# A graph network and expert kernel: the edge loop's drain written out, the operand before the gate, all second expert matrices loaded together

## The reference

```
xn  = layernorm(x)
h   = mish([xn[src], xn[dst], edge_attr] @ W1 + b1)
msg = mish(h @ W2 + b2)
agg = segment_sum(msg, dst)
u   = mish([xn, agg] @ W3 + b3)
y   = xn + u @ W4 + b4
x1  = x + layernorm(y) * gamma + beta
xl  = layernorm(x1)
logits = xl @ gate_weight.T              # 16 experts, top 2, softmax of the two
h_e    = silu(xl @ w1[e].T)              # for the tokens routed to expert e
y_e    = mean over these tokens of h_e, times w2[e].T
out    = x1 + sum over a node's two experts of weight * y_e
```

## Time and profile before

| | |
|---|---|
| median of 3 runs | 1175.64 us (1173.95 to 1177.01) |
| profiled execution | 1175.32 us |
| its span in the profile | 1173.7 us |
| mean granted clock of TensorE | 0.945 |
| TensorE busy | 1059.8 us (90%) |
| VectorE busy | 969.4 us (83%) |
| ScalarE busy | 839.6 us (72%) |
| GpSimd busy | 668.8 us (57%) |

### The profile page before, as it was taken

How to read it: one execution, slowest core, us unless ns; L and a number is a source line. 1 busy time by engine, 2 the same in 40 slices (tenths; PEclk the granted TensorE clock), 3 DMA queues, 4 the chain that set the end, 5 groups by cost and what they waited for, 6 DMA issues and landing times. The chain is left out here.

```text
span 1173.7 us, 19190 instructions
## 1 busy us (share of the span) xinstructions
PE 1059.8 (90%) x5670; PEld 882.1 (75%) x5670; DVE 969.4 (83%) x1646; ACT 839.6 (72%) x1028; POOL 668.8 (57%) x522
## 2 busy tenths in 40 slices
PE   2993999999999999999999999999569997599974
PEld 1772788888888888888888888888347776589962
DVE  6751699999999999999999999999857878773366
ACT  3212799999999999999999999999435454344442
POOL 3245777877877877777777877883321211044310
PEclk9996999999999999999999999999779999789975
DMA  6736766666666666666666666663020311635445
GB/s 179 258 113 147 153 132 131 135 131 133 135 130 131 140 131 131 129 137 131 127 131 133 137 132 126 133 131 101 1 73 10 125 35 53 225 91 152 146 133 170
DMA packets 129067, 148.77 MB, mean 127 GB/s; under 512 B 72573, under 2 KB 81158, under 8 KB 128893
## 3 DMA queue, kind: packets, MB, share of 16 engines
q0 software_dynamic: 38576, 97.54, 38.6%
q1 hardware_dynamic: 90381, 50.03, 16.0%
q10 hardware_dynamic: 16, 0.02, 0.0%
HBM read 137.00 MB, written 15.66 MB: 130 GB/s over the span
## 5 line engine op out<-in xcount | busy, mean ns | idle before, releaser
L944 PE MATMUL ps<-W2h,w1l_w3l 128*128 128x512 f32 x1264 | 425.8, 398 | 0.0
L794 POOL DMA_INDIRECT gath<-dst_table,idx_sl x158 | 262.8, 1663 | 54.0 <-issue 47.4
L944 PEld LDWEIGHTS ps<-W2h,w1l_w3l 128*128 128x128 f32 x1264 | 227.1, 189 | 38.1
L944 PE MATMUL ps<-W2l,w1l_w3l 128*128 128x512 f32 x632 | 247.3, 391 | 0.0
L807 POOL DMA_INDIRECT gath<-src_table,idx_sl x156 | 188.2, 1206 | 100.8 <-issue 52.4
L816 POOL TENSOR_TENSOR msg_lo<-act,msg_hi 128x512 fp32r<-128x512 f32 x79 | 126.0, 1595 | 35.5 <-DVE msg_hi L928 35.5
L944 PEld LDWEIGHTS ps<-W2l,w1l_w3l 128*128 128x128 f32 x632 | 118.8, 188 | 26.4
L878 DVE TENSOR_TENSOR agg<-agg,ps 125x512 f32 x166 | 114.1, 688 | 15.2 <-PE ps L988 10.7
L833 ACT ACTIVATE act<-ps 128x1024 f32<-128x1024 f32 x79 | 81.2, 1027 | 38.4 <-PE ps L976 38.4
L908 DVE SCALAR_TENSOR_TENSOR act<-act,ps 128x1024 f32<-128x1024 f32 x79 | 96.0, 1215 | 2.8 <-ACT act L861 2.8
L890 DVE SCALAR_TENSOR_TENSOR act<-act,ps 128x1024 f32<-128x1024 f32 x79 | 96.0, 1215 | 2.1 <-ACT act L852 2.1
(11 more groups left out here) (345 smaller groups left out, 2363.7 us busy)
## 6 DMA issues: line engine op xcount, KB each, us to landing
w_raw<-in_L_ffn_w_dram SPq DMA_DIRECT2D x25, 512.0 KB, 4.6
ea_sl<-ea_scr SPq DMA_DIRECT2D x158, 64.0 KB, 4.2
ea_scr<-in_edge_attr_dram POOLq DMA_DIRECT2D x1, 5000.0 KB
w_late<-in_L_ffn_w_dram SPq DMA_DIRECT2D x7, 512.0 KB, 6.3
w_raw<-in_L_gnn_W_dram SPq DMA_DIRECT2D x3, 1024.0 KB, 11.5
gath<-src_table,idx_sl POOLq DMA_INDIRECT x158
gath<-dst_table,idx_sl POOLq DMA_INDIRECT x158
x_raw<-in_x_dram SPq DMA_DIRECT2D x5, 448.0 KB
```

What stands on the lines that cost most here:

```text
L794: pool.indirect_dma_start(out=gath[:, k, j, :], out_offset=None, in_=dst_table[:, :], in_offset=bass.IndirectOffsetOnAxis(ap=idx_sl[:, p % ...
L944: return nc.tensor.matmul(ps_2[:, p % 2, j, :], part[:, p % 2, d, j * P:(j + 1) * P], weights[:, d, :], start=False, stop=last)
```

## The change

In the edge phase: the one-hot ring has four slots. VectorE's loop ends after step 79, and the rest of its program is a written list. GpSimd makes no lower half of the last two messages. VectorE makes both halves. The sums of the last three visits go to other banks (two in `ps_2`), so four banks are in use. ScalarE copies the first piece of W3 after the last Exp and the other seven behind its last step. GpSimd makes six remainders of W3, VectorE two.

```diff
+        SUM_BANKS = {PAIRS + 1: (ps_2, 0), PAIRS + 2: (ps_2, 1), PAIRS + 3: (ps_1, PAIRS % 2)}
...
-        act_parts = {PAIRS: (0, 1, 2, 3), PAIRS + 1: (4, 5, 6, 7)}
-        dve_parts = {PAIRS + 4: (0,), PAIRS + 5: (1,), PAIRS + 6: (2,), PAIRS + 7: (3,)}
-        pool_parts = {PAIRS + 3: (4, 5, 6, 7)}
+        DRAIN = PAIRS + 1
+        dve_parts, pool_parts = (0, 1), tuple(range(2, 2 * KC))
...
+            last = PAIRS - 1
+            add_sums(last - 3, 1, second)
+            mark(last - 1)
+            old = last - 2
...
+            nc.vector.tensor_tensor(msg_lo[:, ring(old)][:, 0], act2[:, old % A2, 0], f32(msg_hi[:, ring(old)][:, 0]), ALU.subtract).then_inc(S["msg_lo0_ready"], 1)
+            message(last - 1)
+            dve.wait_ge(S["exp2"], PAIRS)
+            nc.vector.tensor_scalar(act2[:, last % A2], act2[:, last % A2], EXP_MAX, 1.0, ALU.min, ALU.add).then_inc(S["inc2"], 1)
+            split(last - 1)
+            mark(last)
+            add_pair(last - 2)
+            mark(last + 1)
+            mark(last + 2)
+            message(last)
+            split(last)
+            mark(last + 3)
+            add_pair(last - 1)
+            for w in dve_parts:
...
+                nc.vector.tensor_tensor(w3l[:, w, :], w_raw[:, w, :], f32(w3h[:, w, :]), ALU.subtract).then_inc(S["w3_lo"], 1)
+            mark(last + 4)
+            for m in range(last, SUMS):
+                add_pair(m)
```

```diff
-            dve.wait_ge(S["gate_hi"], 1)
-            nc.vector.tensor_tensor(gateT[:, :, 1, :], ps_x[:, 0:KC * E].rearrange("p (q e) -> p q e", e=E), f32(gateT[:, :, 0, :]), ALU.subtract).then_inc(S["gate_lo"], 1)
...
-            dve.wait_ge(S["gb_in"], 32)
...
+                    dve.wait_ge(S["gb_in"], 32)
                     nc.vector.scalar_tensor_tensor(out=yk, in0=yk, scalar=mv[:, 0, 0:1], in1=gamma_b[0:NB, :], op0=ALU.subtract, op1=ALU.mult).then_inc(S["y_scaled"], 1)
```

```diff
+            for part in (gw3a, gw3b):
+                nc.gpsimd.tensor_scalar(part[:], ones[0:ROWS, 0:1].to_broadcast(list(part.shape)), 0.0, None, ALU.mult).then_inc(S["gw_zeroed"], 1)
...
+            sp.wait_ge(S["h_ps"], RT)
+            for e in range(WS, E):
+                sp.dma_start(w2_more[:, e - WS], w2_rows[e]).then_inc(w2_in[e], 16)
...
+                if t in GATES_AT:
+                    part = GATES_AT.index(t)
+                    pe.wait_ge(S["gw_ready"], 1)
...
+                    for k, b in enumerate(GW_PARTS[part]):
+                        ins = nc.tensor.transpose(gw_ps_part(part)[:, k * NB:(k + 1) * NB], gw[:, b, :], ident[0:NB, 0:NB])
...
+            for e in range(E):
+                dve.wait_ge(w2_in[e], 16)
+                dve.wait_ge(S["mean_ps"], e + 1)
+                need(dve, S["y_step"], (e - 1) * KC)
+                for q in range(KC):
+                    nc.vector.tensor_tensor_reduce(out=junk_y[:, e % 2, q, :], in0=w2_tile(e)[:, q, :], in1=ps_n[:, e % 2, 0:FFN], scale=1.0, scalar=0.0,
+                                                   op0=ALU.mult, op1=ALU.add, accum_out=yT[:, q, e:e + 1]).then_inc(S["y_step"], 1)
...
+            for t in range(1, BLOCKS, 2):
+                act.wait_ge(S["res_done"], t + 1)
+                for rows in ROW_PARTS:
+                    act.dma_start(out[t * NB + rows.start:t * NB + rows.stop, :], x1_all[rows, t, :]).then_inc(S["odd_out"], 16)
```

More of the change, by code:

```diff
@@ L812, in _ @@
                 p = s - 4
-                if exists(p):
+                if exists(p) and p < PAIRS - 2:
                     pool.wait_ge(S["msg_hi_ready"], p + 1)
@@ L878, in add_sums @@
                 nc.vector.tensor_tensor(row, row, sums(p)[0:NB, j, :], ALU.add).then_inc(S["summed"], 1)
-            for s in range(FIRST, LAST + 1):
+            for s in range(FIRST, DRAIN):
                 p, r, g, f, m, o = s, s - 1, s - 2, s - 3, s - 4, s - 5
@@ new lines, in message, with split @@
+            def message(f):
+                a3 = act2[:, f % A2]
+                dve.wait_ge(S["quot2"], f + 1)
+                nc.vector.scalar_tensor_tensor(out=a3, in0=a3, scalar=1.0, in1=ps_2[:, f % 2],
+                                               op0=ALU.subtract, op1=ALU.mult).then_inc(S["msg_ready"], 1)
+            def split(f):
+                a3 = act2[:, f % A2]
+                need(dve, S["sum_ps"], ring_free(f))
+                dve.wait_ge(S["msg_ready"], f + 1)
+                nc.vector.tensor_copy(msg_hi[:, ring(f)], a3).then_inc(S["msg_hi_ready"], 1)
+                dve.wait_ge(S["msg_hi_ready"], f + 1)
+                nc.vector.tensor_tensor(msg_lo[:, ring(f)][:, 0], a3[:, 0], f32(msg_hi[:, ring(f)][:, 0]), ALU.subtract).then_inc(S["msg_lo0_ready"], 1)
+                dve.wait_ge(S["msg_lo1_ready"], f)
+                nc.vector.tensor_tensor(msg_lo[:, ring(f)][:, 1], a3[:, 1], f32(msg_hi[:, ring(f)][:, 1]), ALU.subtract).then_inc(S["msg_lo1_ready"], 1)
@@ new lines, in add_pair @@
+            def add_pair(m):
+                for j in range(2):
+                    add_sums(m, j, visit_block(m, j))
+            last = PAIRS - 1
+            add_sums(last - 3, 1, second)
+            mark(last - 1)
+            old = last - 2
+            dve.wait_ge(S["msg_hi_ready"], old + 1)
+            need(dve, S["sum_ps"], ring_free(old))
+            nc.vector.tensor_tensor(msg_lo[:, ring(old)][:, 0], act2[:, old % A2, 0], f32(msg_hi[:, ring(old)][:, 0]), ALU.subtract).then_inc(S["msg_lo0_ready"], 1)
@@ L1342, in _, with gate_transposes @@
         def _(pe):
-            pe.wait_ge(S["gate_in"], 16)
-            for q in range(KC):
-                ins = nc.tensor.transpose(ps_x[:, q * E:(q + 1) * E], gate[:, q * P:(q + 1) * P], ident[0:E, 0:E])
-            ins.then_inc(S["gateT_ps"], 1)
-            pe.wait_ge(S["gate_lo"], 1)
+            def gate_transposes():
+                pe.wait_ge(S["gate_in"], 16)
+                for q in range(KC):
+                    ins = nc.tensor.transpose(ps_x[:, q * E:(q + 1) * E], gate[:, q * P:(q + 1) * P], ident[0:E, 0:E])
+                ins.then_inc(S["gateT_ps"], 1)
             def w1_transposes(*halves):
@@ L1548, in flat, with w2_tile, gw_ps_part, gw3_part @@
             return ap.rearrange("p a b -> p (a b)")
+        def w2_tile(e):
+            return w2_raw[:, e] if e < WS else w2_more[:, e - WS]
+        GW_PARTS = (range(0, 4), range(4, GWB), range(GWB, BLOCKS))
+        def gw_ps_part(n):
+            return (ps_b, ps_m, ps_b)[n][0:E, 0:len(GW_PARTS[n]) * NB]
+        def gw3_part(n, r):
+            tile, first = (gw3a, 0) if n < 2 else (gw3b, GWB)
+            return tile[r:r + E, (GW_PARTS[n].start - first) * NB:(GW_PARTS[n].stop - first) * NB]
+        def gw3_block(t):
+            tile, first = (gw3a, 0) if t < GWB else (gw3b, GWB)
+            return tile[:, (t - first) * NB:(t - first) * NB + NE]
         @block.sync
@@ L1594, in _ @@
                                         in_offset=bass.IndirectOffsetOnAxis(ap=row_i[:, t:t + 1], axis=0)).then_inc(gathered[t % XG], 16)
-            pool.wait_ge(S["h_ps"], RT)
-            for part in (gw3, y3):
-                nc.gpsimd.tensor_scalar(part, ones[0:ROWS, 0:1].to_broadcast(list(part.shape)), 0.0, None, ALU.mult).then_inc(S["out_zeroed"], 1)
-            pool.wait_ge(S["gw3_hi"], 2)
-            nc.gpsimd.tensor_tensor(gw3[64:64 + E, 0:NODES], gwT[:], f32(gw3[0:E, 0:NODES]), ALU.subtract).then_inc(S["gw3_lo"], 1)
+            pool.wait_ge(S["hm_ready"], 1)
+            nc.gpsimd.tensor_scalar(y3, ones[0:ROWS, 0:1].to_broadcast(list(y3.shape)), 0.0, None, ALU.mult).then_inc(S["out_zeroed"], 1)
         @block.scalar
```

157 lines of the change are left out of this document (76 added, 81 removed).

## The result

The changed kernel takes 1166.12 us (median of 4 runs, 1165.20 to 1167.19) against 1175.91 for the kernel before (4 runs on the same chip, 1173.95 to 1177.01): a ratio of 0.9915, 95% interval 0.990 to 0.993. The forecast was 1167.4, with a range of 1161 to 1172. The profiled execution has a span of 1163.5 us, against 1173.7.

The account below looks back on a forecast made before the run. PE was taken to bound the routed tiles, VectorE the last stretch. Terms 0.6 + 2.0 - 2.8 - 1.1 + 1.5 + 6.5 + 1.5 = 8.2 us saved from 1175.3 give 1167.1, as median 1167.4; range 1161 to 1172.

Parts of the forecast that it names:

- the drain: End of the edge loop: VectorE's new written list ends earlier despite collisions with GpSimd; gain 0.6 us.
- the head: Start of the expert phase: GpSimd's clearing of two tables delays VectorE's routing operations; loss 2.8 us.
- the three colliding operations: Drain: two W3 remainders and mark 82 on VectorE alternate with GpSimd's remainders, 1.2 to 1.8 us each.
- ten additions: Drain: the last ten additions stand back to back, 0.90 us apart, and cost 9.0 us.
- rival (d): Drain's written order pays in full, with no collisions there but in the head: 1164.3 us; chance 0.12.
- Node phase: Its start: without the wait for beta and the gate's load, the first product comes earlier; gain 2.0 us.
- the second clearing: Expert phase's start: the third routing operation meets GpSimd's clearing of the smaller table, for 0.4 us more.
- Tiles: Routed tiles: ten transposes of the gate weights move into the loop, where PE has no idle time; loss 1.1 us.
- Scaling: Scaling of the sums before the outputs: clearing no longer meets it, 1.67 becomes 0.17 us; gain 1.5 us.
- outputs: Reductions of 16 experts without the copy and its wait: 1.435 us each, 23.0 instead of 29.5; gain 6.5 us.
- stores: Kernel's end: issuing the 20 stores from two queues instead of one; gain 1.5 us.
- Rival (c): Outputs: the twelve later matrices, queued at once, load slowly, making the kernel slower; 1179 us at 180 GB/s; chance 0.04.

Follow-up runs that it names:

- e_pool8: The changed kernel with all eight remainders of W3 on GpSimd and none on VectorE: 1168.58 us, ratio 0.9937 to the kernel before.
- e_gate: The changed kernel with the gate's transposes, copy, remainder and the wait for gamma and beta ahead of the first block again: 1168.02 us, ratio 0.9937.
- e_clear3: The changed kernel with the larger table cleared three times in a row: 1168.62 us, ratio 0.9935.
- e_memset: The changed kernel with both tables cleared by a fill (memset) that reads no SBUF: 1163.32 us, ratio 0.9894.
- e_best: The changed kernel with four PSUM banks for the means, tables cleared by memset, all W3 remainders on GpSimd: 1163.07 us, ratio 0.9893.
- e_copy: The changed kernel with the copy per expert and the wait behind it put back in the outputs: 1170.62 us, ratio 0.9953.
- e_banks: The changed kernel with the means of four experts in four PSUM banks instead of two: 1164.94 us, ratio 0.9914.
- e_onequeue: The changed kernel with all twenty stores issued by SyncE again: 1166.48 us, ratio 0.9913.
- e_fixed: The changed kernel with the last ten additions going to one fixed block, no block number read: 1165.67 us, ratio 0.9910.
- e_apart: The changed kernel with the last ten additions going to two fixed blocks in turn, each waiting only for the one before its predecessor: 1167.05 us, ratio 0.9923.

## Why the prediction was right

The sum was 8.2 us and the span fell by 10.2. The two terms that were off by more than 1 us, the drain and the head, were both forecast too low in gain (1.1 and 1.3); 0.9 went the other way at the loop's end. The total stayed in the range because no error was large, not because they cancelled.

**Drain: 0.6 forecast, 1.7 measured.** The mechanism held step by step. On the clock of the kernel before (0.86 earlier), Exp started at 829.8 (forecast 829.85), bounding at 830.85 (830.95), the last split ended at 839.2 (839.3). Mis-sized was the rest: pair 77 was added by 841.05, not 841.6 (0.5); the three colliding operations took 4.52, not 4.7 (0.2 to 0.3 with rounding); ten additions took 8.78, not 9.0 (0.2). Missed was GpSimd, which would have held the next phase from 0.3 us on. So rival (d)'s 3 us could not have paid in full. Without collisions GpSimd's own remainders would be shorter too (1.27 us each in `e_pool8`, 1.43 here), an estimate of 1 us for six, which leaves some 1.3 of the 3.

**Node phase: 2.0 forecast, 2.4 measured,** 1.93 of it at the first product (8.49 to 6.56 us after the start), the mechanism as forecast. `e_gate` takes that away again. The size is in part luck of this one trace: the twelve kernels with this start average 152.7 us for the phase, which is 1.8 less than the kernel before.

**Head: -2.8 forecast, -1.5 measured.** This is the step that failed in size: "finds GpSimd already running ... So it ends about 2.4 us late". It ended 0.82 late, and the second clearing cost under 0.1 and not 0.4. I had read one case, the scaling of the sums, as "waits until GpSimd's running one ends". `e_clear3` shows one stop of 0.7 to 0.8 per clearing. Why the scaling lost 1.48 under a clearing of 1251 columns, which it met 1.4 us after that one's start, stays open. With the fill 0.94 us of the head come back; the 0.6 left (30.30 against 29.70) are not the clearing's. They are mostly TensorE's clock, a term that the prediction did not have. Within the routing VectorE needs the count of tokens per expert, which TensorE makes in two pairs of small products. Timelines of TensorE and VectorE, first of `e_memset`, then TensorE's of `e_best`:

```profile
1014.87 0.58 PE L1882 MATMUL f_ps_m<-msum,tri 125*125 125x16 f32 x2
...
1015.49 0.17 DVE L1768 COPY cnt<-f_ps_m 128x16 f32<-128x16 f32 x1 [0.51 <-PE f_ps_m L1882]
```

```profile
1015.85 0.37 PE L1885 MATMUL f_ps_m<-msum,tri 125*125 125x16 f32 x2
```

In twelve of the fourteen traces the pairs take 0.61 and 0.58 us and VectorE stands idle for 0.51. In the kernel before and in `e_best` they take 0.40 and 0.37 (granted clock 0.96 and 0.93 over the 4 us around them) and VectorE does not wait. `e_best` has the same fill as `e_memset` and a head of 29.81: of the 0.6, 0.5 goes with this wait. The three heads of 31.7 have one more wait for TensorE, of 0.42 to 0.54 us, 29.3 us into the head. The clock alone does not explain that one: over the 6 us around it it is 0.84 to 0.85 there, but 0.83 in the changed kernel (31.24), which does not wait.

**Tiles: -1.1 forecast, -0.9 measured.** Ten transposes at 0.11 start to start make 1.1, as forecast. The comparison is fair only because both kernels lost about as much to the clock: it averages 0.83 over the first 10 us of tiles in each. With the fill it is 1.00 there and the tiles take 83.37 with the same transposes, less than the 83.77 before. The clock behind the head is worth 1.3 us, and the prediction did not have it.

**Scaling 1.5, outputs 6.5, stores 1.5: measured 1.48, 6.17, 1.78.** Two experts take 2.93 us, not 2.87, because the handover leaves TensorE 0.17 and 0.37 us idle in turn where 0.06 was taken. `e_copy` and `e_banks` show what set the old pace and what sets the new one. Rival (c) was refuted by one row: 350 GB/s, and no wait of VectorE for a matrix. On the stores the Trainium skill (DMA: Bandwidth & Descriptors, "Issuing engines are not separate DMA queues") says that a second issuing engine saves only the time of issue. Here that time is what bound the tail: 8.71 us for twenty stores in one queue, 6.66 and 6.45 for ten in each of two, and 1.7 to 1.8 us of tail in these traces (0.9 against the longest tail with two queues). So the rule holds, and the 0 us that I drew from it for this term does not.

**The spread of the node phase.** It is between 151.8 and 154.3 us long with the same code and the same start (first product at 6.56 in each of twelve traces), as large as the terms argued over here. TensorE's clock makes most of it. Windows of 6 us, from 7 us after the phase's start, of the kernel after and of `e_onequeue`:

```profile
863.10:869.10 6.00, 6.00 (x23) 4.69 (x23) 3.12 (x4) 1.00 (x3) 1.45 (x2) 0.68 0.17 52
```

```profile
861.84:867.84 6.00, 6.00 (x16) 4.44 (x16) 2.07 (x4) 1.10 (x3) 1.45 (x1) 0.51 0.24 60
```

TensorE is fully busy in both, but the clock rises from 1.2 to 2.4 GHz at different points, and it does 23 products or 16. Over the twelve traces the granted clock of this window goes from 0.72 down to 0.50, and the first output product comes later each time, from 23.9 to 25.1 us after the phase's start, without one exception. From there to the end of the last output product it is 107.3 us in eight of them (and in the kernel before and `e_gate`), and 108.1 to 108.3 in `e_copy`, `e_onequeue`, `e_fixed` and `e_apart`. In these four the clock has already fallen 124 to 126 us after the phase's start (0.75 to 0.90), in all others it is 1.00 there.

**What stays open.** Why the clock rises and falls at other points in other executions is not shown, nor what makes the tail differ by 0.8 us. For these reasons effects under some 2 us are claimed from stages and not from medians.

## What to carry to other kernels

When a stage ends in a barrier, work out the end of every engine, and take GpSimd's from what follows it and not from its rows: shortening VectorE's list by 1.0 and by 2.7 us was worth 0.3 here, and moving two operations from it to GpSimd lost 1.3. A small clearing placed at the head of a chain of VectorE operations costs its stop, and in this kernel slower first tiles behind it; with a fill that has no input neither was seen. When the same stage differs between two traces, compare the granted clock in it first. And a wait for the instruction just before, once per expert or per addition, is a price to look for in the gaps of the bounding engine (0.34 us with a copy, 0.19 to 0.30 per addition).

## What the runs showed that I had not expected

- GpSimd needs 7.00 us from the end of its last subtraction by the row to its next phase, with six and with eight subtractions alike, where VectorE needs 0.98.
- The same program reaches the full clock in the node phase sooner or later, and the first output product moves with it by 1.2 us; a wait for four small products made the head 0.5 us longer at the lower clock.
- A GpSimd clearing of 1001 columns that reads SBUF (2.75 us) stops a two-input VectorE operation once, for 0.7 to 0.8 us, near its own beginning; a fill of the same columns takes 0.93 us and stops nothing.
- A dependent addition costs 0.19 us more than an independent one, and 0.11 more with its address in a register. A block number costs 0.24 us to read if nothing hides it (2.41 us for ten).
- With the fill the head was 0.94 us shorter, and another 1.33 us came off the tiles, where the granted clock was 1.00 instead of 0.69 in a stretch of 4 us.
